# GpSimd waits for landed rows between the batches of a gather, and once between scatters, in a four-layer transformer kernel

## The reference

```
def _L1_ffn_ref(x, router_w, gate_w, up_w, down_w, s_gate_w, ...):     # 2048 tokens, 8 experts of width 352
    probs = softmax(x @ router_w.T)
    topk_w, topk_idx = top_k(probs, 2)                                  # each token goes to 2 experts
    topk_w = topk_w / sum(topk_w)
    moe_out = sum over experts: combine[:, e] * (silu(x @ gate_w[e]) * (x @ up_w[e])) @ down_w[e]
    shared = (silu(x @ s_gate_w + s_gate_b) * (x @ s_up_w + s_up_b)) @ s_down_w + s_down_b
    return moe_out + shared
x = x + tanh(g_ffn[1]) * _L1_ffn_ref(_layernorm(x), ...)
```

## Time and profile before

| | |
|---|---|
| median of 3 runs | 1060.24 us (1059.17 to 1061.88) |
| the profiled execution's own time | 1052.42 us |
| its span | 1050.7 us |
| PE busy | 925.3 us (88%) |
| POOL busy | 519.2 us (49%) |
| 32 scatters, first start to last start | 693.33 to 738.59 |
| 32 gathers, first start to last start | 970.88 to 1009.98 |
| granted TensorE clock, mean of the span | 0.968 of full speed |

### The profile page before, as it was taken

How to read it: one execution, slowest core, us unless ns; L and a number is a source line. 1 busy time by engine, 2 the same in 40 slices (tenths; PEclk the granted TensorE clock), 3 DMA queues, 4 the chain that set the end, 5 groups by cost and what they waited for, 6 DMA issues and landing times. The chain is left out here.

```text
span 1050.7 us, 16731 instructions
## 1 busy us (share of the span) xinstructions
PE 925.3 (88%) x5123; PEld 411.4 (39%) x5124; DVE 696.9 (66%) x1384; ACT 553.1 (53%) x848; POOL 519.2 (49%) x550
## 2 busy tenths in 40 slices
PE   0476889998799899999998998999899999999758
PEld 0333444443333233333322233534355555565313
DVE  6989979997896866777678747874324544332157
ACT  5999979897377677666576725343211111111110
POOL 1212547753245756765666711047278879400730
PEclk9987899999999999999999998999999999999969
DMA  8997446666354334323212429978579988565953
GB/s 324 349 246 198 108 95 106 115 121 120 105 137 97 87 105 101 78 63 89 61 47 78 67 87 211 335 243 275 177 159 223 229 203 197 136 127 167 355 160 120
DMA packets 254672, 165.57 MB, mean 158 GB/s; under 512 B 192596, under 2 KB 221268, under 8 KB 253832
## 3 DMA queue, kind: packets, MB, share of 16 engines
q1 hardware_dynamic: 245656, 135.64, 50.8%
q0 software_dynamic: 8080, 27.60, 8.1%
q10 hardware_dynamic: 864, 1.44, 0.4%
HBM read 74.47 MB, written 45.47 MB: 114 GB/s over the span
## 5 line engine op out<-in xcount | busy, mean ns | idle before, releaser
L1840 DVE CUSTOM_DVE_ANT_0 ajunk<-p_row,mask_row 128x512 bf16<-128x512 f32 x256 | 166.2, 685 | 64.8 <-PE p_row L1664 57.2
L1575 ACT ACTIVATE prob<-p_pair,mask_col,any_key 128x512 f32<-128x512 f32 x168 | 122.0, 774 | 65.6 <-PE p_pair L1719 65.2
L1664 PE MATMUL p_row<-ks,early_place 99*128 99x512 f16 x256 | 98.1, 385 | 15.0 <-DVE top L1840 14.2
L1719 PE MATMUL p_pair<-early_place,ks 101*128 101x512 f16 x256 | 97.2, 384 | 6.1 <-ACT prob L1575 4.8
L3055 DVE SCALAR_TENSOR_TENSOR shid<-p_pair,ssilu 128x352 f32<-128x352 f32 x36 | 18.9, 525 | 95.8 <-PE p_pair L2945 95.8
L1575 ACT ACTIVATE early_place<-p_pair,mask_col,any_key 128x512 f32<-128x512 f32 x88 | 64.0, 775 | 28.4 <-PE p_pair L1719 28.3
L2960 PE MATMUL s_down<-mw,shT 128*128 (+5 forms) x396 | 75.8, 379 | 1.0 <-DMA shT<-shidr 1.0
L2874 ACT ACTIVATE ssilu<-s_gate 128x352 f32<-128x352 f32 x36 | 16.7, 465 | 108.1 <-PE s_gate L2945 108.1
L2862 POOL DMA_INDIRECT mw<-y_slots,dest x32 | 30.6, 957 | 73.1 <-DMA y_slots<-spare 63.7
L613 PE MATMUL po<-w2T,ctxT 128*128 128x512 f16 x256 | 57.7, 379 | 3.6 <-DMA ctxT<-w 3.6
L1416 POOL TENSOR_TENSOR o<-raw_o,rec 128x512 f32<-128x512 f32 x15 | 20.1, 1341 | 78.6 <-DMA rec<-inv_d 78.6
(11 more groups left out here) (447 smaller groups left out, 2195.1 us busy)
## 6 DMA issues: line engine op xcount, KB each, us to landing
x_slots<-nought SPq DMA_DIRECT2D x6, 1536.0 KB, 13.6
y_slots<-spare SPq DMA_DIRECT2D x36, 256.0 KB, 2.5
early_place<-in_ctx SPq DMA_DIRECT2D x8, 1024.0 KB, 5.4
early_place<-halves_d SPq DMA_DIRECT2D x45, 128.0 KB, 2.5
halves_d<-halves SPq DMA_DIRECT2D x18, 256.0 KB, 2.0
x<-in_x SPq DMA_DIRECT2D x4, 1024.0 KB, 7.9
w<-in_L_ffn_w SPq DMA_DIRECT2D x1, 4096.0 KB
w<-in_L_ffn_w SPq DMA_DIRECT2D x4, 1024.0 KB
```

Of the source, the lines that this page charges most:

```text
L1575: nc.scalar.activation(prob_of(KB * blk + k, pr)[:, c, :], p_col[c][:], ACT.Exp, bias=mask_col[:, b, k:k + 1], scale=any_key[:, b:b + 1]). ...
L1664: nc.tensor.matmul(p_row[n % 2][:], qs[0:ROWS_R, j, g, t * P:(t + 1) * P], ks[b % 2][0:ROWS_R, g, :], start=True, stop=True).then_inc(t_ro ...
L1719: nc.tensor.matmul(p_col[c][:], ks[b % 2][0:ROWS_C, g, k * P:(k + 1) * P], qs[0:ROWS_C, j, g, :], start=True, stop=True).then_inc(t_col, 1)
L1840: nc.vector.tensor_tensor_reduce(junk[:, n % 2, :], p_row[n % 2][:], mask_row[:, blk // HPG, :], 1.0, -3e38, ALU.add, ALU.max, top[blk % 2 ...
```

## The change

Two conditional waits are added on POOL, nothing else:

```
--- before.py
+++ after.py
@@ -2311,6 +2311,8 @@
                 for s in range(2):
                     nc.gpsimd.indirect_dma_start(out=x_slots, out_offset=bass.IndirectOffsetOnAxis(ap=dest[:, s, t:t + 1], axis=0),
                                                  in_=row_of(t), in_offset=None).then_inc(done, 16)
+                if t == LATE_B * TPB - 1:
+                    pool.wait_ge(m_scat_mid, SCATTERED)
             pool.wait_ge(m_wl, NSP + len(ORDER))
@@ -2862,6 +2864,8 @@
                     nc.gpsimd.indirect_dma_start(out=gathered[:, t, s, :], out_offset=None, in_=y_slots,
                                                  in_offset=bass.IndirectOffsetOnAxis(ap=dest[:, s, t:t + 1], axis=0)
                                                  ).then_inc(e_tile[t % TPB] if t // TPB == LATE_B else e_gathered[t // TPB], 16)
+                if t < LATE_B * TPB and t % TPB == TPB - 1:
+                    pool.wait_ge(e_gathered[t // TPB], 16 * 2 * TPB)
```

## The result

After: 1041.97 us in the median of 4 executions (1039.54 to 1044.08). Before, on the same chip: 1059.7 us (1058.86 to 1061.88). The ratio is 0.984 (95% interval 0.981 to 0.987), so the change takes 17.7 us off there. The profiled execution of after took 1040.38 us (span 1038.6), against 1052.42 us before: 12.0 us less.

The account below looks back on a forecast made before the run. It took PE's stall under the later gathers to bound the kernel. 21.2 us from the gathers and 3.2 from the scatters, at most 24.4, were cut to 16, giving 1044.2 us; 8-in-10 range 1036 to 1067.

Parts of the forecast that it names:

- relief: Likeliest case: pauses remove PE's stall under the gathers; minus 16 us, between minus 4 and minus 24, chance 0.50.
- What bounds the kernel: Gathers' stretch: PE stands from 991.7 with late reports to ACT and DVE; this stall is what the change can move.
- The stall gone: Gathers' stretch to the end: PE ends at 1023.9 instead of 1047.3, DVE at 1027.0 instead of 1048.2, 21.2 us earlier.
- The deduction of a third: Two thirds of at most 24.4 us taken, 16 us, since later gather batches may each start with a debt.
- The pauses, 6.4, 2.6 and 2.6 us: POOL's waits after the 8th, 16th and 24th gather; they make the last gather 11.6 us later.
- price of 2.3 us: Time from a gather's issue to its landing with nothing in front, read from the last gather of the kernel before.
- The end set by `combine_late`: End of the program: the last late tile waits for its gathers until 1024.8 and ends at 1027.0.
- The later gathers alone cost nothing, cover 21 us, as long as the stall stays: Gathers land at 1012.2 and 1017, against `combine(2)` at 1033.52 and `combine_late(0)` at 1038.95: no cost.
- rival without effect: Stall not POOL's: 1060; or only in recorded executions: timed runs plus 2.3 us, 1062.5. Chance 0.29.
- The rival on the other side (the stall follows the gathers): PE stands until 3 us after the last landing, about 1027.4; plus 7 us, 1067, between plus 3.5 and 11.5; chance 0.21.
- The scatters: Pause after the 16th scatter: covered, costs nothing; gives 3.2 us if 16 in a row don't raise the small stall.
- The Trainium skill's rule: Engine and DMA ports of SBUF are disjoint; by it the pauses give nothing, 0 instead of 16 us.

Follow-up runs that it names:

- first comparison: Kernel before against the whole change, timed beside each other on a chip not identified: 1059.7 and 1041.97 us, ratio 0.984.
- lagged kernel: Changed kernel, but gather waits are for the batch before the one just issued, so POOL never stops; 1027.49 us on chip B, 1056.7 on C, ratio 1.000 each.
- gather waits alone: Changed kernel without its wait between the scatters, the three waits between gathers kept; 1041.95 us on chip B, ratio 1.012 to the kernel before.
- single wait: Changed kernel with one landing wait only, after the second gather batch, none in the scatters; 1028.28 us on chip B (1.001), 1031.52 on D (1.000).
- scatter wait alone: Changed kernel without its gather waits, only the wait between the scatters kept; 1053.1 us on chip C, ratio 0.997 to the kernel before.
- pauses without a landing: Changed kernel with six waited-for fills of an unused tile replacing each of three landing waits; chip B: 1039.53 us (1.011), again 1039.08 (1.010).

## Why the prediction was right, and where it was not

The predicted 1044.2 us is 2.2 us from the measured 1041.97 and relief was the likeliest case. Step by step:

- **What bounds the kernel (PE, stalled under the gathers): right, on the chips that have the stall.** In all four stalled traces it runs from 20 to 22 us after the first gather to 5.3 to 5.9 us after the start of the last. (The prediction's "some 3 us after the last one" holds for the last landing, not for the last issue.) What the prediction took for a property of the program is one of program and chip: on B and D the kernel before takes 1029 to 1030 us, 26 less than on C.
- **The stall gone, worth 21.2 us at most: right in size.** PE ended at 1025.5, forecast 1023.9. From the first gather to the start of the last product before has 61.6 us (first comparison) and 63.7 (C); after has 41.1 and 38.3, and the lagged kernel on B 38.9. So the stall is worth 20.5 us (first comparison) to 25.4 us (C), and the pauses remove all of it.
- **The deduction of a third, for a stall that comes back in later batches: wrong.** Nothing came back (48 matmuls in each 10 us). What kept the gain small was another term.
- **The pauses, 6.4, 2.6 and 2.6 us: mis-sized, and this is the step that failed.** They measured 8.6, 4.4 and 4.2 us, on C 7.7, 5.3 and 4.4. The sum is 17.2 us instead of 11.6. Two readings went wrong. The price of 2.3 us came from the earlier trace rows, the last gathers of before, behind which some 0.45 MB were left to move (91 GB/s over the 5 us of the earlier trace rows). It nearly holds for as much: 2.87 and 2.81 us in the runs with one wait, where POOL's queue q0 moves 0.45 and 0.42 MB during the pause. In every run with waits after batches 1 and 2, the pauses of 4.2 to 5.6 us have 1.0 MB of gathers still to move at their start (in one case 0.74 MB, and 0.45 MB of a store). The queues in the second pause of the gather waits alone (999.47 to 1004.61), then in the pause of the single wait on B (987.78 to 990.64):

```profile
q0 software_dynamic: 307, 1.00, 59.7%
q1 hardware_dynamic: 18, 0.02, 1.3%
...
q0 software_dynamic: 144, 0.45, 48.5%
```

  The store that the `combine` before it releases, 1.0 MB, has moved while the 8 gathers were being issued (q1 1.02 MB from 989.0 to 999.5), and the gathers only 1.1 of their 2.1 MB. That the store is what leaves this backlog is argued from these bytes; the store wasn't taken away in any run. The first pause had been sized by 2.12 MB in q0 by 986.6, but 13 gathers had been issued by then, so these bytes were not batch 0's alone. In after, with 8 issued, q0 has moved 1.98 MB at the same distance from the first gather, and the last of the 2.10 MB come up to 2.7 us later.
- **The end set by `combine_late`: right, and 9.2 us later than forecast** (DVE's end at 1036.2 instead of 1027.0). The last gather of the third late tile starts at 1024.66 instead of 1018.75, 5.9 us; it lands 6.83 us after that, not 3.25 (3.6 us more); DVE needs 4.7 us behind it, not 5.0. Of these 5.9 us a part is not pause but issue: POOL's rows of the gathers that it writes while a `combine` runs on DVE are longer (see the last section).
- **The median.** The two errors partly cancel: a full 21.2 us of relief less 9.2 is 12.0 us, which is what the profiled executions differ by, while the prediction took two thirds of 24.4 (21.2 and the scatters' 3.2), 16 us. The medians differ by 17.7 us in the first comparison and by 14.6 on C. In the first, the profiled execution of before was 7.3 us below its own median, and no view here says in which stage. The closeness of 1044.2 is partly luck.
- **"The later gathers alone cost nothing, cover 21 us, as long as the stall stays": right, with the condition.** Without the stall the cover is small. The prediction gave this case as plus 2.3 us, under the rival without effect; on B the gather waits alone cost 12.3. That 10 us is, for the most part, the same mis-sized term.
- **The rival without effect: fell on the stalled chips, and its second half came true elsewhere**, since on B the stall isn't there and the gather waits make the kernel slower, by five times what was worked out. **The rival on the other side (the stall follows the gathers): fell.** In neither trace of the changed kernel from a comparison that has the stall is there a gap in PE's rows under the gathers.
- **The scatters: cost nothing, right; a gain of up to 3.2 us, not shown.** The pause was 2.32 us in after, PE's chunks stood 2.59 us apart throughout, and the next stage began at 761.63, as before (761.48). But the gap of the earlier trace rows is absent also from before on C, so its absence in after proves nothing. In the lagged kernel on C the gap is 0.5 us, and with the scatter wait alone there is none.
- **The Trainium skill's rule** ("SBUF — State Buffer", section "SBUF: two separate sides", that compute and transfers can't slow each other): on B the runs agree, with PE at 48 matmuls in 10 us next to DMA engines 92% busy. On C PE falls to 4 in 10 us next to the same gathers, with the DMA engines *less* busy (0.73), and keeps its 48 in the run whose gathers pause. So the rule may well hold and something else couple GpSimd's gathers to PE on some chips, or the recording of the execution play a part (see what stays open); read as a forecast that the pauses give nothing, it failed.

**What stays open.** The cause of the stall. It sets in after some 16 gathers without a pause, it delays the reports of finished work to ACT and DVE as well as PE's issue, it ends 5 us after the last gather is issued, and it depends on the chip, or on the time at which it was used. Neither the string of gathers nor the traffic is enough to make it, since the lagged kernel on B has both, at a higher DMA share, without it.

One rival of the prediction was never tested: that the stall is there only in an execution that is recorded. Every execution here, the timed ones too, comes with a recorded span and clock. Counted in the stored traces, the number of DMA landing records leaves this open and may point to it. It is 9844 in every trace from B and D, 8950 to 9067 in the four stalled ones, and 9476 and 9437 in the changed kernel of the first comparison and on C. All but a few tens of the missing ones belong to the stretch of the scatters (690 to 760) and the one from 960 on: 378 and 301 records there in before on C, 747 and 768 in the lagged kernel on B. So whatever loses records under POOL's strings is at work where the stall is, and on those chips also where it isn't, in the changed kernel. Which is cause and which effect isn't shown. If recording is the cause, the gain belongs to recorded executions alone.

Whether it takes the landing or only the pause to prevent it, and how few pauses do, would need the single wait and the pauses without a landing on a chip like C. For the same reason no version is shown to beat both kernels everywhere. The single wait after the second batch is the candidate: it costs nothing on B and D, while the three gather waits cost 1.2% on B. On a chip like C it could give at most the stall, 24.8 us (79.5 less 54.7).

How much pause is free can be estimated from the table. Where the gathers set the end, DVE ends 8.1 to 9.4 us after the last gather starts (66.1 less 58.0, 63.3 less 53.9). Without stall the tail takes 54.5 us, so the last gather may start up to 45 or 46 us after the first, 5 us later than without pauses (40.4). The single wait uses 3 to 4 of them, where the three gather waits take 17.

## What to carry to other kernels

Single matmuls with "issue" ahead of them in the middle of a chunk, together with consumers that take finished work many microseconds late, are a coupling and not a dependency. Pausing the engine that issues the long string of indirect DMAs is worth a try, but time the unchanged kernel on several chips first, since the stall may be the chip's and the pause is a pure cost where there is none.

Price a wait for landing by what the queue still has to move when the wait begins, and count what else was moved while the batch was being issued: the figure from the last gathers, with 0.45 MB left (2.3 us), came close where as much was left (2.8 us) and was 2 to 3 us short with 1.0 MB left (4.2 to 5.6 us).

When a stall is removed, work out the path of the next engine with the same care as the gain. Here the transfers that had 21 us of cover became the end of the program.

## What the runs showed of the hardware that was not expected

- One program differs by 26 us (2.5%) between chips, 1029 to 1030 us on B and D and 1056 us on C. By the traces of before on C and the lagged kernel on B, 24.8 us of it lie between the first gather and DVE's end. The granted clock doesn't explain it, since PE's clock falls to 0.50 (the 1.2 GHz level) only after PE has stopped being fed, and is back when the work is.
- On such a chip 32 indirect DMAs, one each 1.25 us, leave PE 4 to 7 matmuls in 10 us after the first 20 us; pauses of 4 to 9 us after each 8 prevent it completely.
- A gather that POOL writes out while DVE runs a `combine` takes it longer. It is 0.94 or 0.95 us in nearly every row without one beside it (all 27 from the sixth on in the lagged kernel on C, where the first `combine` starts after the last gather), and mostly 1.0 to 1.4 us beside one: 1.34 at 1002.97 in after, with a `combine` from 1002.73. A pause isn't what does it, since the first gather behind one takes 0.94 at 988.23, before the `combine` of 989.73. It adds some 2 us to the delay of the last gather in after. Why the two engines touch isn't shown.
